# Second LayerNorm of three batches by channel instead of by token, in a fused WKV and MLP kernel

## The reference

```python
def _layernorm(x, axis=-1, eps=1e-05):
    m = jnp.mean(x, axis=axis, keepdims=True)
    v = jnp.var(x, axis=axis, keepdims=True)
    return (x - m) / jnp.sqrt(v + eps)
...
# a recurrence over the tokens, per channel, with k = layernorm(x), v = context
def _L0_ffn_ref(x, W0, bias0, W1, bias1):
    X = x.reshape(-1, H).astype(jnp.float16)
    D = jnp.dot(X.astype(jnp.float32), W0.T) + bias0
    D = jax.nn.gelu(D, approximate=False).astype(jnp.float16)
    E = jnp.dot(D.astype(jnp.float32), W1.T) + bias1
    return E.astype(jnp.float16).reshape(B, L, H)
x = x + jnp.tanh(g_xattn[0]) * _L0_xattn_ref(4, 1024, 1024, w, u, _layernorm(x, axis=-1), ctx_2048)
x = x + jnp.tanh(g_ffn[0]) * _L0_ffn_ref(_layernorm(x, axis=-1), W0, bias0, W1, bias1)
```

## Time and profile before

| what | value |
|---|---|
| time, median of 3 runs | 1995.39 us (1993.98 to 1995.86) |
| the profiled execution: its time, its span | 1994.41 us, 1992.6 us |
| TensorE (PE) busy | 93% of the span |
| VectorE (DVE), ScalarE (ACT), GpSimd (POOL) busy | 43%, 28%, 13% |
| DMA, mean share of the 16 engines | 40.5% in the queue that SP issues to |
| mean granted TensorE clock | 0.993 of full speed |

### The profile page before, as it was taken

One profiled execution on the slowest core, in us unless ns is written; L12 is line 12 of the kernel. 1 busy time (PEld: TensorE's weight loads), 2 busy tenths in 40 slices (PEclk: granted clock), 3 DMA queues, 4 the chain that ended last, 5 costly groups with the idle time before them and its releaser, 6 DMA issues.

```text
span 1992.6 us, 20961 instructions
## 1 busy us (share of the span) xinstructions
PE 1856.8 (93%) x8960; PEld 878.9 (44%) x8960; DVE 847.7 (43%) x998; ACT 549.8 (28%) x647; POOL 261.9 (13%) x202
## 2 busy tenths in 40 slices
PE   0069998899999999999999999999999999999999
PEld 0034444344544444444444444444444444444444
DVE  6978779686433666631223776642111000000000
ACT  3139744434422433410001443420100221210000
POOL 2335411334330011000000101000000000000000
PEclk9989999999999999999999999999999999999999
DMA  5727837578353442442233334323322222123330
GB/s 195 253 81 277 313 132 266 209 252 311 115 177 138 143 161 96 142 182 98 93 127 122 114 129 164 137 96 116 127 92 87 96 85 85 64 85 127 127 116 32
DMA packets 76748, 287.12 MB, mean 144 GB/s; under 512 B 7920, under 2 KB 7920, under 8 KB 69488
## 3 DMA queue, kind: packets, MB, share of 16 engines
q1 hardware_dynamic: 75648, 285.24, 40.5%
q10 hardware_dynamic: 1008, 0.55, 0.1%
HBM read 218.66 MB, written 67.11 MB: 143 GB/s over the span
## 4 chain that ended last, share of the span: by engine, by line
PE 81%; DVE 10%; issue 3%; DMA 3%; ACT 2%; POOL 1%; SPq 0%; ACTq 0%; DVEq 0%; POOLq 0%
PE acc L658 43%; PE acc L636 35%; DVE S L525 3%; PE front L608 1%; DVE stats L456 1%; DMA W<-parts_dram 1%; DVE S L511 1%; DVE S L514 1%; PE front L585 1%; PE back L617 1%; ACT L380 1%; POOL X L328 1%; DMA xin<-x_in 1%; DVE xin L472 1%; DMA b<-bias_in 1%
## 5 line engine op out<-in xcount | busy, mean ns | idle before, releaser
L636 PE MATMUL acc<-XT,W 128*128 128x512 f16 x4096 | 900.3, 381 | 17.5 <-DMA W<-parts_dram 12.0
L658 PE MATMUL acc<-DT,W 128*128 128x512 f16 x4096 | 892.5, 379 | 0.0
L636 PEld LDWEIGHTS acc<-XT,W 128*128 128x128 f16 x4096 | 401.6, 98 | 495.9 <-issue 13.6
L658 PEld LDWEIGHTS acc<-DT,W 128*128 128x128 f16 x4096 | 400.1, 98 | 471.6
L536 DVE SCALAR_TENSOR_TENSOR xo<-e,tg,xo 128x512 f32<-128x512 f16 x64 | 50.0, 783 | 654.3 <-ACT e L419 654.3
L411 ACT ACTIVATE DT<-acc,b 128x512 f16<-128x512 f32 x256 | 175.7, 687 | 546.1 <-PE acc L636 545.6
L419 ACT ACTIVATE e<-acc,b 128x512 f16<-128x512 f32 x64 | 43.9, 686 | 616.8 <-PE acc L658 616.8
L525 DVE RECIPROCAL S<-front 128x512 f32<-128x512 f32 x62 | 207.5, 3347 | 0.0
L328 POOL TENSOR_TENSOR X<-X,S 128x512 f32<-128x512 f32 x64 | 77.6, 1213 | 641.3 <-DVE S L528 641.3
L509 DVE TENSOR_TENSOR front<-front,V 128x512 f32<-128x512 f32 x62 | 43.2, 696 | 203.6 <-ACT front L380 203.6
L456 DVE BATCH_NORM_STATS2 stats<-front 128x6 f32<-128x512 f32 x64 | 41.4, 688 | 198.0 <-PE front L608 198.0
(11 more groups left out here) (50 smaller groups left out, 617.0 us busy)
## 6 DMA issues: line engine op xcount, KB each, us to landing
W<-parts_dram SPq DMA_DIRECT2D x56, 2048.0 KB, 8.5
parts_dram<-W SPq DMA_DIRECT2D x64, 512.0 KB, 6.1
stage<-w_in SPq DMA_DIRECT2D x52, 512.0 KB, 6.0
xin<-x_in SPq DMA_DIRECT2D x32, 512.0 KB, 6.1
V<-vT_in SPq DMA_DIRECT2D x64, 256.0 KB, 5.0
X<-xT_in SPq DMA_DIRECT2D x64, 256.0 KB, 3.0
x_dram<-X SPq DMA_DIRECT2D x32, 512.0 KB, 3.9
xo<-x_dram SPq DMA_DIRECT2D x32, 512.0 KB, 4.1
```

Source lines behind the costliest of these rows:

```text
L636: mm = nc.tensor.matmul(acc[m % BANKS][:, :], W[:, (nb // Q) % 2, part, nb % Q, P * c:P * (c + 1)], XT[:, c, HALF * half:HALF * (half + 1) ...
L658: mm = nc.tensor.matmul(acc[m % BANKS][:, :], W[:, s % 2, part, q, P * c:P * (c + 1)], DT[:, nb, HALF * half:HALF * (half + 1)], start=(nb ...
```

## The change

Batches 1 to 3 lose `tokens_x2`, `post`, `channels_x2` and `copy_xt`; batch 0 keeps them. In their place, for each half of a batch (512 tokens), and with the channels left on the partitions:

- GpSimd sums the eight units of a half into `total` as they come, seven adds of 128x512 (in `residual`).
- TensorE multiplies `total` with `share`, a 128x128 matrix whose elements are all 1/1024 (`means`): one f32 matmul 128x512, whose output has the mean of each token on every partition.
- VectorE subtracts it from the eight slots of `X2` (`centre`), ScalarE squares them (`square`), VectorE sums the squares (`add_square`), TensorE makes the variance in the same way (`variances`).
- VectorE adds EPS (`variance`), GpSimd raises the 128x512 result to the power -0.5 (`deviation`), and VectorE multiplies (`scale`) and writes `XT` in f16.

`load_xT` gets eight semaphores in place of four, and so waits for a residual four units older; for batches 2 and 3 it waits for `scaled` in place of `x2t_done`. The first unit of batch 2 or 3 on TensorE waits for `dev_ready`, and the first matmul of a batch after 0 for `scaled`. The diff, without declarations, the counts of `s_pool0` and the calls in the loops of the slots:

```diff
-    for i in range(TILES):
-        LN2_SLOT[TILES + i] = (88 + 2 * i, 90 + 2 * i)
+    for h in range(2):
+        MEAN_SLOT[2 + h] = 88 + 14 * h
...
-        for i in range(TILES):
-            LN2_SLOT[T + i] = (at + 72 + 6 * i, at + 75 + 6 * i)
+        for h in range(2):
+            MEAN_SLOT[2 * (b + 1) + h] = at + 72 + 18 * h
...
+VAR_AFTER, SCALE_AFTER = 7, 9
+MEAN_AT = {k: half for half, k in MEAN_SLOT.items()}
+VAR_AT = {k + VAR_AFTER: half for half, k in MEAN_SLOT.items()}
+CENTRE_AT = {k + 1 + i: (half, i) for half, k in MEAN_SLOT.items() for i in range(CB // 2)}
+SCALE_AT = {k + SCALE_AFTER + i: (half, i) for half, k in MEAN_SLOT.items() for i in range(CB // 2)}
...
-                if n >= 4:
-                    sp.wait_ge(x2_done, n - 3)
+                if n >= 8:
+                    sp.wait_ge(x2_done, n - 7)
                 if b:
-                    sp.wait_ge(x2t_done, TILES * (b - 1) + HT * (i // CB + 1))
+                    if b == 1:
+                        sp.wait_ge(x2t_done, HT * (i // CB + 1))
+                    else:
+                        sp.wait_ge(scaled, UNITS * (b - 2) + CB * (i // CB + 1))
...
+                c = n % CB
+                if n >= UNITS and c:
+                    half = n // CB
+                    pool.wait_ge(x2_done, n + 1)
+                    if c == 1 and half >= 4:
+                        pool.wait_ge(scaled, CB * (half - 3))
+                    if c > 1:
+                        pool.wait_ge(sum_done, (CB - 1) * (half - 2) + c - 1)
+                    nc.gpsimd.tensor_tensor(total[:, half % 2, :], X2[:, n % UNITS - 1, :] if c == 1 else
+                                            total[:, half % 2, :], slot, ALU.add).then_inc(sum_done, 1)
+            def deviation(half):
+                pool.wait_ge(dev_ready, half - 1)
+                nc.gpsimd.tensor_tensor(total[:, half % 2, :], total[:, half % 2, :],
+                                        power[:, :].to_broadcast([P, HALF]), ALU.pow).then_inc(dev_done, 1)
...
+            def square(half, c):
+                act.wait_ge(centred, CB * (half - 2) + c + 1)
+                if half > 2 or c >= 2:
+                    act.wait_ge(added, CB * (half - 2) + c - 1)
+                nc.scalar.activation(front[1][:, c % 2, :], X2[:, CB * (half % 2) + c, :], ACT.Square)\
+                    .then_inc(squared, 1)
...
+            def centre(half, c):
+                b = half // 2
+                slot = X2[:, CB * (half % 2) + c, :]
+                if c == 0:
+                    dve.wait_ge(mean_done, half - 1)
+                    dve.wait_ge(x2_stored[b % 2], 16 * CB * (b // 2 + 1))
+                nc.vector.tensor_tensor(slot, slot, front[0][:, 0, :], ALU.subtract).then_inc(centred, 1)
+            def add_square(half, c):
+                dve.wait_ge(squared, CB * (half - 2) + c + 1)
+                if c == 0:
+                    if half > 2:
+                        dve.wait_ge(var_done, half - 2)
+                    nc.vector.tensor_copy(squares, front[1][:, 0, :]).then_inc(added, 1)
+                else:
+                    dve.wait_ge(added, CB * (half - 2) + c)
+                    nc.vector.tensor_tensor(squares, squares, front[1][:, c % 2, :], ALU.add).then_inc(added, 1)
+            def variance(half):
+                dve.wait_ge(var_done, half - 1)
+                nc.vector.tensor_scalar(total[:, half % 2, :], front[0][:, 1, :], EPS, None, ALU.add)\
+                    .then_inc(dev_ready, 1)
+            def scale(half, c):
+                b, h = divmod(half, 2)
+                if c == 0:
+                    dve.wait_ge(dev_done, half - 1)
+                    dve.wait_ge(mm_done, GROUPS * (b - 1) + GROUPS1)
+                nc.vector.tensor_tensor(XT[:, c, HALF * h:HALF * (h + 1)], X2[:, CB * h + c, :],
+                                        total[:, h, :], ALU.mult).then_inc(scaled, 1)
...
+            def means(half):
+                pe.wait_ge(sum_done, (CB - 1) * (half - 1))
+                pe.wait_ge(y_done, UNITS * (half // 2 + 1))
+                if half % 2:
+                    pe.wait_ge(dev_ready, half - 2)
+                nc.tensor.matmul(front[0][:, 0, :], share[:, :], total[:, half % 2, :], start=True, stop=True)\
+                    .then_inc(mean_done, 1)
+            def variances(half):
+                pe.wait_ge(added, CB * (half - 1))
+                nc.tensor.matmul(front[0][:, 1, :], share[:, :], squares, start=True, stop=True)\
+                    .then_inc(var_done, 1)
```

More of the change, by code:

```diff
@@ L35 @@
 LN2_SLOT = {}
+MEAN_SLOT = {}
+VAR_AFTER, SCALE_AFTER = 7, 9
 def place_front():
@@ L102, in sems @@
             return [sem(f"{name}{i}") for i in range(n)]
+        share = sb("share", [P, P])
         ident, ident16 = sb("ident", [P, P]), sb("ident16", [P, P], F16)
@@ L115, in build @@
         xh = sb("xh", [P, H], F16)
+        total = sb("total", [P, 2, HALF])
+        squares = xh[:, :].bitcast(F32)
         V = sb("V", [P, 2, HALF])
@@ L134, in build @@
         s_const, s_pool0, s_dve0, s_act0 = (sem(f"s_{n}") for n in ("const", "pool0", "dve0", "act0"))
-        x_landed, v_landed, xT_landed = sems("x_landed", HT), sems("v_landed"), sems("xT_landed", 4)
+        x_landed, v_landed, xT_landed = sems("x_landed", HT), sems("v_landed"), sems("xT_landed", 8)
         x2_stored, xo_landed, out_stored = sems("x2_stored"), sems("xo_landed"), sems("out_stored")
@@ L144, in build @@
         x2t_done, xt_done, xt_copied = sem("x2t_done"), sem("xt_done"), sem("xt_copied")
+        sum_done, mean_done, centred, squared, added, var_done, dev_ready, dev_done, scaled = (
+            sem(n) for n in ("sum_done", "mean_done", "centred", "squared", "added", "var_done", "dev_ready",
+                             "dev_done", "scaled"))
         hi_done, ws_done, lo_done = sem("hi_done"), sem("ws_done"), sem("lo_done")
@@ L174, in load_xT @@
                 b, i = divmod(n, UNITS)
-                if n >= 4:
-                    sp.wait_ge(x2_done, n - 3)
+                if n >= 8:
+                    sp.wait_ge(x2_done, n - 7)
                 if b:
-                    sp.wait_ge(x2t_done, TILES * (b - 1) + HT * (i // CB + 1))
+                    if b == 1:
+                        sp.wait_ge(x2t_done, HT * (i // CB + 1))
+                    else:
+                        sp.wait_ge(scaled, UNITS * (b - 2) + CB * (i // CB + 1))
                     sp.wait_ge(x2_stored[(b - 1) % 2], 16 * CB * ((b - 1) // 2 + 1))
-                sp.dma_start(X2[:, i, :], xT[b, i]).then_inc(xT_landed[n % 4], 16)
+                sp.dma_start(X2[:, i, :], xT[b, i]).then_inc(xT_landed[n % 8], 16)
             def store_x2(n):
@@ L307, in _ @@
             nc.gpsimd.memset(power[:, :], -0.5).then_inc(s_pool0, 1)
+            nc.gpsimd.memset(share[:, :], 1.0 / H).then_inc(s_pool0, 1)
             nc.gpsimd.iota(negt[:, :], [[-P, TILES]], base=0, channel_multiplier=-1,
@@ L310, in _ @@
             nc.gpsimd.memset(state[:, 0:CB, :], SEED).then_inc(s_pool0, 1)
-            pool.wait_ge(s_pool0, 4)
+            pool.wait_ge(s_pool0, 5)
             nc.gpsimd.affine_select(out=ident[:, :], in_=ident[:, :], compare_op=ALU.not_equal, fill=1.0,
                                     base=0, pattern=[[-1, P]], channel_multiplier=1).then_inc(s_pool0, 1)
-            pool.wait_ge(s_pool0, 5)
+            pool.wait_ge(s_pool0, 6)
             nc.gpsimd.tensor_copy(ident16[:, :], ident[:, :]).then_inc(s_pool0, 1)
@@ L325, in residual @@
                 pool.wait_ge(y_done, n + 1)
-                pool.wait_ge(xT_landed[n % 4], 16 * (n // 4 + 1))
+                pool.wait_ge(xT_landed[n % 8], 16 * (n // 8 + 1))
                 slot = X2[:, n % UNITS, :]
                 nc.gpsimd.tensor_tensor(slot, slot, S[:, n % 2, 1, 0:HALF], ALU.add).then_inc(x2_done, 1)
+                c = n % CB
[12 more added lines that the diff above has]
+                                        power[:, :].to_broadcast([P, HALF]), ALU.pow).then_inc(dev_done, 1)
             def lo_piece(g):
@@ L353, in _ @@
                         residual(n)
+                    if K in VAR_AT:
+                        deviation(VAR_AT[K])
                     if b == 0 and 1 <= k <= NB - 2 * Q:
@@ L435, in _ @@
                         copy_xt(X2_AT[K])
+                    if K in CENTRE_AT:
+                        half, i = CENTRE_AT[K]
+                        square(half, 2 * i)
+                        square(half, 2 * i + 1)
                     if k < GROUPS1:
@@ L476, in norm_x @@
                     dve.wait_ge(s_dve0, 2)
-                    dve.wait_ge(s_pool0, 6)
+                    dve.wait_ge(s_pool0, 7)
                 nc.vector.scalar_tensor_tensor(row, grow[:, :], negt[:, T % TILES:T % TILES + 1], row,
@@ L572, in _ @@
                         post(X2T_AT[K])
+                    if K in CENTRE_AT:
+                        half, i = CENTRE_AT[K]
+                        for c in range(2 * i, 2 * i + 2):
```

(26 more changed lines are left out.)

## The result

The changed kernel takes 2210.1 us (median of 4 runs, 2209.1 to 2211.2) against 1995.6 us: a ratio of 1.108, 95% interval 1.106 to 1.110. It is 214.5 us slower, far outside the forecast range of 1944 to 2040 us.

A forecast was written before the change was run, and what follows sets the result against it. TensorE's own instruction stream and what stops it bound the kernel. 1994.4 - 31.7 (transposes) + 9.6 (f32 matmuls) - 11 (weight waits and clock) = 1961.3 us, so 1962 as the median; range 1944 to 2040 us.

The forecast's parts named there:

- T: Duration of GpSimd's 128x512 power in `deviation`, run six times: taken as 20 us, between ends of 1.6 and 256.
- rival 3: T over 48 us: VectorE waits at `scale`, TensorE at `variances` and its banks; 2039 us at T = 61; chance 0.29.
- the formula: Loss from the six powers: (T-27) + 2(T-41) + (T-58) + 2(T-61) us, each term from zero up.
- room: Time a power may take before TensorE stops: 27 and 58 us in batch 0, 41 and 61 in batches 1 and 2.
- VectorE's chain: In batch 0, products, output additions and the next half's operations follow the power before TensorE's `variances`; room 27 us.
- TensorE's stream: Transposes removed in batches 1 to 3 save 31.7 us; twelve f32 matmuls at 0.8 us add 9.6; net -22.1 us.
- SP's queue: Eight semaphores let SP issue weight parts earlier, cutting TensorE's 12.0 us of waits and slow clock behind: -11 us.
- the bound of -16: Most that the earlier weight loads could gain: 12.0 us of TensorE's waits and 4.0 of clock.
- costed at nothing: GpSimd's added sums run beside VectorE at no cost; centring, squares and products are hidden; a 20 us power loses nothing.
- the 19 us of VectorE behind the power: Batch 0: 8 products, two output additions and 16 operations of the next half, between the power and `variances`.
- rival 2: The power outlasts its cover a little, T from 27 to 48 us: between 1962 and 1994 us; chance 0.08.

The follow-up runs named there:

- e5: Changed kernel with GpSimd's wide power at another size in each of the six halves, from one column to 256; a single run of 1956.6 us.
- e7: Changed kernel with the power on the first 128 of 512 columns only; 1956.6 us, ratio 0.981 to the kernel before.
- e2: Changed kernel with GpSimd's wide power made an add of the same operands, all waits kept; 1956.4 us, ratio 0.980 to the kernel before.
- e6: Changed kernel with full powers, but VectorE's waiting `scale` moved to slots behind the power's end; 2095.0 us, ratio 1.050 to the kernel before.
- e4: Changed kernel with the power replaced by a square root on ScalarE and a reciprocal on VectorE; 1956.4 us, ratio 0.981 to the kernel before.
- e8: Changed kernel with root and reciprocal for the power, and X2's loads back on four semaphores; 1972.6 us, ratio 0.989 to the kernel before.
- e1: Kernel before with eight semaphores instead of four for X2's loads, nothing else changed; 1978.3 us, ratio 0.992.

## Why the prediction was wrong, point by point

- **The step that failed is the size of one term: T, the power's duration, taken as 20 us between ends of 1.6 and 256.** It measured 82.2. Of the 0.55 us of one column 0.39 is start-up and 0.16 recurs for every column (e5). The geometric middle was a guess between ends a factor 160 apart; the prediction said that T decides, and its rival 3 (chance 0.29) is what came, but it took 61 us as the last value worth holding in the range. With T = 21 us its time comes out (e7), and with an add in the power's place (e2) the whole loss is gone.
- **A second step failed: the path by which the power stops TensorE. With T = 82.2 the formula gives 55 + 82 + 24 + 42 = 204 us, 2166 us in all. 44 more were measured.** A room is T less the wait: 29 and 28 us for batch 0's powers, 44 and 59 in batches 1 and 2; forecast were 27, 58, 41 and 61. Three are near, though only the last by the mechanism named, so that is in part luck. In batch 0 the reason given was VectorE's chain, and it was GpSimd's weight pieces, queued behind the power on the same engine (e6). The prediction named who waits for the power and left GpSimd's own queue out; that is the 58 against 28, 30 us. In batches 1 and 2 the first stop came by SP's store of `xo` and the weights behind it, not by `variances`. The 44 us are these 30 and some 20 of the clock, less 6 by which the rest of the forecast was too high.
- **Not in the formula: the clock.** TensorE waited 234.3 us, but 2209.4 - 1954.0 (the spans of the changed kernel and of e4) = 255.4 us. Of the other 21 us some 20 are slower matmuls behind the waits, nearly 3 us to each of the seven; the 16 of 1103.91 lost 2.8, the 80 of 571.85 lost 2.6. The prediction used this effect for before's waits and left it out of its formula.
- **Right: TensorE's stream.** 31.7 us out, 0.86 us a matmul in against 0.8 taken: -21.4 net; e8 shows -21.7.
- **Right in its mechanism: SP's queue.** -11 was forecast for TensorE's waits on the weight parts and the clock behind them; the stretch they lie in lost 9.5 us in e1. The last parts went at 345.9 rather than 349 to 350, the middle loads left no wait at all, and 4.2 us of 12.0 remain. But the whole of e1 is -16.8, beyond the bound of -16: the other 7 us are small waits elsewhere that the prediction didn't have.
- **Right while the power is short: what was costed at nothing.** Sums on GpSimd, centring, squares and eight products: e2 and e4 show no new wait of TensorE. The forecast, which had the power at nothing, was 1962; 1956.4 was measured, and the queue's 16.8 for 11 makes up the difference. Only the 19 us of VectorE behind the power were too low (28.5 in e7), which a longer power brings out.
- **Two slips without effect.** L332, read as an add, is a subtraction with an f16 operand. At T = 48 the formula gives 1997 us, where rival 2 ends at 1994.

## What to carry to other kernels

An operation that the trace shows only at one column says little of its price at 512: measure it alone at two sizes before it goes on a busy queue. Of a long operation ask first what is queued behind it on its own engine, then what is queued behind each instruction that waits for it, through the transfer queue too; here no matmul of the changed kernel ever waited for the product that the power feeds, and the stops came from weight pieces, stores and accumulator banks. If it can't be made short, move the waiting instruction, not only the operation (e6: 115 us), and if another pair of engines has it in 5 us, as root and reciprocal do, take those (e4).

## What the runs showed of the hardware

- GpSimd's power costs 0.16 us a column plus 0.39 us (e5), and for 128 columns the same on 16 partitions as on 128; its add costs 0.002 us a column, a factor of 80. The Trainium skill ("GPSIMD Engine Reference", Engine selection) has GpSimd about 2x slower than VectorE for an elementwise add, multiply or maximum of two inputs. The traces are not far from that, with 1.09 to 1.26 us for an add of 128x512 against 0.70 for L509 on VectorE; the rule doesn't speak of the power.
- GpSimd's subtractions for the weight pieces slow VectorE, and its power doesn't. In e4 three XT products beside weight pieces take 7.70 us, against 1.29 for two without. In e6, inside two powers which follow each other from 1010.13 for 163.84 us, the output additions keep their 0.75 us, which became 2.62 beside weight pieces in e7, and eight XT products take 4.90 us, 0.61 each (VectorE's timeline):

```profile
1013.53 0.75 DVE L618 SCALAR_TENSOR_TENSOR xo<-e,tg,xo 128x512 f32<-128x512 f16 x1 [3.48 <-ACT e L463]
1027.35 0.75 DVE L618 SCALAR_TENSOR_TENSOR xo<-e,tg,xo 128x512 f32<-128x512 f16 x1 [13.06 <-ACT e L463]
...
1098.80 4.90 DVE L610 TENSOR_TENSOR XT<-X,total 128x512 f16<-128x512 f32 x8
```

Both kinds have two operands in SBUF. Why the one kind of GpSimd operation hinders and the other doesn't was not tested.
